# One tile of 1024 columns for the two exponent banks of a sequence, and new orders of the steps on four engines

## What is computed

```python
xn = layernorm(x)
z, xBC, dt = split(xn @ W_in)                   # 512, 768, 8 columns
dt = softplus(dt + dt_bias)
xBC = silu(causal_conv(xBC, conv_w, conv_b))    # 4 taps along the tokens
x_, B, C = split(xBC)                           # 8 heads of 64; state of 128
# per chunk of tokens, L[t, s] = exp(sum of dt*a between s and t), 0 for s > t
Y_diag = (C B^T * L) @ (x_ * dt)                # inside a chunk
Y_off  = C @ state * exp(cumsum)                # from the chunks before
y = (Y_diag + Y_off + x_ * D) * silu(z)
y = rmsnorm(y) * rms_w
h = xn + y @ W_out
out = x + layernorm(h) * ln_g + ln_b + tanh(xn @ F1 @ F2 @ F3 + bias)
```

## Time and profile before

| | before |
|---|---|
| median of 3 runs | 858.38 us (854.18 to 859.85) |
| the profiled execution | 857.2 us, its span 855.5 us |
| PE busy | 800.8 us, 94% |
| DVE busy | 726.5 us, 85% |
| ACT busy | 681.3 us, 80% |
| POOL busy | 702.0 us, 82% |
| mean granted TensorE clock | 0.976 |

### The profile page before, as it was taken

How to read it: one execution, slowest core, us unless ns; L and a number is a source line. 1 busy time by engine, 2 the same in 40 slices (tenths; PEclk the granted TensorE clock), 3 DMA queues, 4 the chain that set the end, 5 groups by cost and what they waited for, 6 DMA issues and landing times.

```text
span 855.5 us, 18389 instructions
## 1 busy us (share of the span) xinstructions
PE 800.8 (94%) x4944; PEld 671.5 (78%) x4944; DVE 726.5 (85%) x1826; ACT 681.3 (80%) x1767; POOL 702.0 (82%) x1096
## 2 busy tenths in 40 slices
PE   1479999999999999999999999999999999999974
PEld 1368888888888888888888888888888888888753
DVE  1669899998999999899999999999999998998741
ACT  1169888898888888988888889888888898888841
POOL 4036888898888889988888899888888988888884
PEclk9689999999999999999999999999999999999986
DMA  5000000000000000000000000000000000000000
GB/s 174 0 1 13 14 26 26 26 11 14 25 25 25 25 25 25 6 19 25 25 25 25 25 25 1 24 25 25 25 25 25 25 0 24 25 25 13 14 13 25
DMA packets 20848, 19.98 MB, mean 23 GB/s; under 512 B 2646, under 2 KB 20568, under 8 KB 20824
## 3 DMA queue, kind: packets, MB, share of 16 engines
q1 hardware_dynamic: 20824, 19.71, 7.2%
HBM read 11.31 MB, written 8.39 MB: 23 GB/s over the span
## 4 chain that ended last, share of the span: by engine, by line
POOL 39%; DVE 25%; issue 17%; PE 13%; ACT 2%; SPq 2%; POOLq 1%; DVEq 1%; DMA 0%; ACTq 0%
DVE u L624 7%; POOL xw L446 7%; PE ring L1012 5%; POOL obuf L491 4%; POOL left L434 3%; POOL sdec L453 3%; POOL xd L461 3%; POOL rs L483 3%; DVE pa L646 3%; POOL right L430 3%; DVE lay L677 3%; POOL obuf L493 3%; POOL btg L441 2%; DVE lay L683 2%; PE yoff_bank L1149 2%
## 5 line engine op out<-in xcount | busy, mean ns | idle before, releaser
L624 DVE SCALAR_TENSOR_TENSOR u<-ring,cw,u 128x256 f32<-128x256 f32 x576 | 260.5, 469 | 30.4 <-ACT u L847 29.8
L1012 PE MATMUL ring<-xhl,wh 128*128 128x262 f32 x768 | 174.8, 319 | 3.4 <-DVE u L624 3.4
L1012 PE MATMUL ring<-wh,xhl 128*128 128x512 f32 (+1 forms) x512 | 164.1, 374 | 3.3 <-DVE u L624 3.3
L1012 PEld LDWEIGHTS ring<-xhl,wh 128*128 128x128 f32 x768 | 124.7, 193 | 43.6 <-DVE u L624 21.6
L847 ACT ACTIVATE u<-ring,cb,cw 128x256 f32<-128x256 f32 x192 | 107.9, 562 | 45.6 <-PE ring L1012 40.9
L907 ACT ACTIVATE xdt<-xsb,dts 128x64 f32<-128x64 f32 x512 | 128.5, 335 | 0.0
L1131 PE MATMUL yd_bank<-xdt,lay 128*128 128x64 f32 x1024 | 123.2, 274 | 0.9 <-ACT yts L916 0.9
L1149 PE MATMUL yoff_bank<-wo,yts 128*128 128x256 f32 x512 | 122.1, 382 | 1.1 <-ACT yts L916 0.7
L1131 PEld LDWEIGHTS yd_bank<-xdt,lay 128*128 128x128 f32 x1024 | 121.2, 194 | 1.7 <-ACT yts L916 1.3
L1012 PE MATMUL ring<-xhl,wl 128*128 128x262 f32 x384 | 110.2, 287 | 0.0
L1012 PEld LDWEIGHTS ring<-wh,xhl 128*128 128x128 f32 x512 | 93.9, 192 | 20.0 <-issue 7.2
(11 more groups left out here) (134 smaller groups left out, 1995.7 us busy)
## 6 DMA issues: line engine op xcount, KB each, us to landing
xin<-in_x_dram SPq DMA_DIRECT2D x32, 256.0 KB, 2.9
out_dram<-obuf SPq DMA_DIRECT2D x32, 256.0 KB, 2.8
lay<-in_w_in_dram SPq DMA_DIRECT2D x1, 1288.0 KB
wo<-in_w_out_dram SPq DMA_DIRECT2D x1, 512.0 KB
lay<-in_f1t_dram SPq DMA_DIRECT2D x1, 256.0 KB
lay<-in_f2t_dram SPq DMA_DIRECT2D x1, 256.0 KB
lay<-in_f_dram SPq DMA_DIRECT2D x1, 256.0 KB
lng<-in_ln_g_dram SPq DMA_DIRECT2D x1, 128.0 KB
```

Source lines behind the costliest of these rows:

```text
L624: v.scalar_tensor_tensor(out=u[:, ct], in0=conv_bank(ct)[:, :, t:t + P], scalar=cw[:, ct, t:t + 1], in1=u[:, ct], op0=ALU.mult, op1=ALU.ad ...
L1012: last = mul(out, a, c, start=first and i == 0, stop=i == n - 1)
```

## The change

The two banks become one PSUM tile `e_pair` of 2 x 512 columns. `exponents` fills both halves and signals once, `decay` is one exponential over 1024 columns, `weigh` is one instruction over 1024 columns, and each waits for the whole pair. The semaphores have one instance per sequence in place of two. All four `one_pass` functions list their steps in a new order. No other instruction is added or taken away.

```diff
+        e_pair = ctx.enter_context(nc.psum_tensor("e_pair", [P, 2, 512], F32))
+        e_bank = [e_pair[:, 0], e_pair[:, 1]]
...
-                v.scalar_tensor_tensor(out=mm[:, q, hs], in0=e_bank[half][:, :].rearrange("p (j t) -> p j t", t=P), scalar=1.0,
-                                       in1=btg[:, q, P:2 * P].unsqueeze(1).to_broadcast([P, 4, P]),
-                                       op0=ALU.min, op1=ALU.mult).then_inc(m_done[q][half], 1)
+                v.scalar_tensor_tensor(out=mm[:, q], in0=e_pair[:, :, :].rearrange("p a (j t) -> p (a j) t", t=P), scalar=1.0,
+                                       in1=btg[:, q, P:2 * P].unsqueeze(1).to_broadcast([P, H, P]),
+                                       op0=ALU.min, op1=ALU.mult).then_inc(m_done[q], 1)
...
-                s.activation(e_bank[half][:, :], e_bank[half][:, :], ACT.Exp).then_inc(e_done[q][half], 1)
+            def decay(k, q):
+                act.wait_ge(e_in_psum[q], k + 1)
+                s.activation(e_pair[:, :, :], e_pair[:, :, :], ACT.Exp).then_inc(e_done[q], 1)
...
                 if begun(k - 1 + q):
-                    pe.wait_ge(m_done[1 - q][half], k + q)
-                bank = e_bank[half]
-                mul(bank[:, :], left[:, 2 * q + half], right[:, :, :].rearrange("p j t -> p (j t)"), start=True, stop=True)\
-                    .then_inc(e_in_psum[q][half], 1)
+                    pe.wait_ge(m_done[1 - q], k + q)
+                for half, bank in enumerate(e_bank):
+                    last = mul(bank[:, :], left[:, 2 * q + half], right[:, :, :].rearrange("p j t -> p (j t)"), start=True, stop=True)
+                last.then_inc(e_in_psum[q], 1)
...
                 pe.wait_ge(xdt_done[q], k + 1)
+                pe.wait_ge(m_done[q], k + 1)
                 for h in range(H):
-                    if h % 4 == 0:
-                        pe.wait_ge(m_done[q][h // 4], k + 1)
...
             def one_pass(k, b):
-                b1, bo = (b + 1) % BUF, (b - 1) % BUF
+                b1, b2, bo = (b + 1) % BUF, (b + 2) % BUF, (b - 1) % BUF
                 if live(k - 1):
                     scale_x(k - 1, 1)
-                if live(k + 1):
-                    halo(k + 1, b1)
+                if live(k):
+                    residual(k, b)
+                    residual_bias(k, b)
+                    spread_rows(k)
```

More of the change, by code:

```diff
@@ L216, in program @@
                 "mv2_done", "ve2_done", "rs2_done", "shift2_done", "hn_done", "hg_done", "out_done"))
-        e_in_psum, e_done, m_done = ([sems(f"{n}{q}_", 2) for q in range(Q)] for n in ("e_in_psum", "e_done", "m_done"))
+        e_in_psum, e_done, m_done = (sems(n, Q) for n in ("e_in_psum", "e_done", "m_done"))
         def begun(step):
@@ L528, in one_pass @@
                 if live(k):
-                    skip_x(k, 1)
+                    mask_g(k, 0)
+                    decay_state(k, b, 0)
                     add_skip(k, 0)
@@ L535, in one_pass @@
                     mask_g(k, 1)
+                if live(k - 1):
+                    last_norm_scale(k - 1, 0)
+                if live(k):
+                    skip_x(k, 1)
             passes(pool, one_pass)
@@ L669, in low_rows, with weigh @@
                 last.then_inc(rows_done, 1)
-            def weigh(k, q, half):
-                dve.wait_ge(e_done[q][half], k + 1)
+            def weigh(k, q):
+                dve.wait_ge(e_done[q], k + 1)
                 dve.wait_ge(g_done[q], k + 1)
@@ L751, in one_pass @@
                 if live(k):
-                    tap(k, 5, 2)
+                    softplus(k, b, 6)
+                    softplus(k, b, 7)
+                    softplus(k, b, 8)
                 if live(k + 1):
@@ L929, in one_pass @@
                 if live(k):
+                    conv_in(k, 4)
+                    conv_silu(k, b, 0)
+                if live(k - 2):
+                    last_apply(k - 2, 1)
+                if live(k - 1):
+                    b_and_g(k - 1, 1)
+                if live(k):
                     conv_in(k, 5)
-                    conv_silu(k, b, 0)
                 if live(k - 1):
@@ L952, in one_pass @@
                     branch(k + 1, 0)
+                    softplus_exp(k + 1)
+                if live(k - 1):
+                    y_channels(k - 1, 0)
                 if live(k):
@@ L957, in one_pass @@
                 if live(k - 1):
-                    y_channels(k - 1, 0)
+                    square(k - 1, 0)
+                if live(k - 2):
+                    last_apply(k - 2, 0)
                 if live(k + 1):
-                    softplus_exp(k + 1)
                     conv_in(k + 1, 0)
@@ L1174, in one_pass @@
                 if live(k - 2):
-                    transpose_y(k - 2, 1)
+                    out_project(k - 2, 1)
                 if live(k - 1):
-                    y_off(k - 1, bo, 0)
+                    x_tokens(k - 1, bo, 1)
                 if live(k):
@@ L1199, in one_pass @@
                     sums(k)
+                    x_tokens(k, b, 0)
                 if live(k + 1):
```

234 lines of the change are left out of this document (94 added, 140 removed).

## The result

The changed kernel takes 868.90 us in the median (867.65 to 869.51, 4 runs), the kernel before in the same comparison 856.77 (854.18 to 859.85): a ratio of 1.0138, interval [1.0098, 1.0179]. Its profiled execution took 868.63 us.

A forecast was written before the change was run, and what follows sets the result against it. The prediction took a chain of waits through POOL, ACT, PE and DVE, with DVE's stands on the shared port, to set a pass of 24.85 for 24.48 us; 857.2 + 0.37 x 31 gave 868.7, some 869 us, range 847 to 890.

The forecast's parts named there:

- the term of the sum: Growth of one pass from 24.48 to 24.85 us, +0.37 us, counted 31 times as +11.5 us.
- the walk: Nine steps once round the chain of waits, from POOL's `ve` through ACT, DVE and PE back to POOL: 24.85 us.
- Step 6: On DVE, `sv` meets POOL's `decay_state` and stands until 17.15; with `ww` and `pa` done at 17.75 us.
- Step 8: On DVE, `weigh`, held 0.1 by `mask_g`, ends at 23.2; `last_h` of sequence 1 and its statistics at 24.05 us.
- Step 9: On DVE, `pa` stands on POOL's `add_skip` until 24.3; with it, `mv` and the handover to POOL, 24.85 us.
- the two stands on the port: DVE's `sv` and `pa` waiting for large POOL instructions: 0.6 and 0.4 us of the pass, 23.85 without them.
- POOL's sum of 24.35: POOL's own instructions in the new order without the wait for `mv`: 24.35 us a pass, 0.13 less than before.
- steps 3 and 4: PE's six steps done at 9.7 us, then ACT's work from `branch` to `conv_in(0)` done at 13.5 us.
- The merge: One exponential on ACT and one weighing on DVE in place of two each: counted at 0 for the time.
- POOL alone: Rival: both stands of DVE fall away and POOL's own work sets the pass, -4 us, 853 us; chance 0.33.
- The shorter ends: Rival: waits outside the full passes shrink by some 10 us, with POOL's 24.35 in the loop, 843 us; chance 0.17.
- The third: Rival: each softplus of a DVE block waits anew, one more large POOL instruction per pass, 900 us; chance 0.08.

The follow-up runs named there:

- e2: Changed kernel with POOL's `mask_g` of sequence 0 moved ahead of `scale_x` of sequence 0: 863.62 us.
- e9: e2 with POOL's `decay_state(k-1, 1)` moved behind `layer_norm_scale(k+2)`: 862.82 us.
- e10: e9 with DVE's `last_mean_var(k-2, 1)` moved ahead of `softplus(k, b, 5)`: 860.33 us.
- e1: Changed kernel with the merge undone, two exponentials and two weighings per sequence again, in the new orders: 869.81 us.
- e5: Kernel before, in its old orders, with the merged exponential and weighing alone: 857.66 us.
- e12: e8 with the merged exponential and weighing added: 852.65 us in the median of nine executions.
- e8: Kernel before with POOL's `mask_g(k, 1)` moved ahead of `output(k-1, 1)`, into the wait for `last_apply`: 846.48 us, ratio 0.9871.
- e6: Changed kernel with the edits of e2 and e3 together, early mask and spread softplus: 870.66 us.
- e3: Changed kernel with DVE's softplus block (`sv`, `ww`, `pa`) taken apart and spread between the taps: 866.08 us.
- e11: e10 with POOL's `mask_g(k, 1)` moved into its wait for `last_apply`, and ACT's `b_and_g(k-1, 1)` ahead of `last_apply(k-2, 1)`: 848.56 us, ratio 0.9903.
- e4: Changed kernel with ACT's `last_apply(k-2, 1)` moved behind `conv_in(k, 5)`: 877.46 us.
- e7: e6 with POOL's `mask_g(k, 1)` moved into its wait for `last_apply`, and ACT's `b_and_g(k-1, 1)` ahead of `last_apply(k-2, 1)`: 856.87 us.

## Why the prediction was right, and where it was not

The time (869 for 868.9), the sign and the term of the sum, 0.37 us a pass, came out, and so did the walk's places. The causes put on the term did not, so that its size is luck in part. Counted from `ve` at 439.17 in the changed kernel's trace, forecast and measured:

| step | forecast | measured |
|---|---|---|
| 1, `conv_in(5)` done | 2.8 | 2.73 |
| 2, taps of tile 5 done | 4.3 | 4.29 |
| 3, PE done with what ACT's last branch needs | 9.7 | 9.70 |
| 4, ACT's `conv_in(0)` done | 13.5 | 13.45 |
| 5, statistics of sequence 0 done | 16.55 | 16.53 |
| 6, `sv`, `ww`, `pa` done | 17.75 | 17.54 |
| 7, DVE ready for `weigh` | 22.0 | 21.82 |
| `mask_g(0)` done | 22.1 | 22.02 |
| 8, statistics of sequence 1 done | 24.05 | 24.21 |
| 9, POOL's `ve` | 24.85 | 24.76 |

**Step 6** gave 0.6 us of the loss to `sv` on `decay_state`. The stand is there, from 455.62 to 456.30, with POOL's `sdec` ending at 456.27, and it costs nothing: after steps 6 and 7 DVE is ready 0.2 us before the mask, which ends where POOL's own row lengths put it. The prediction's own figures say so too: its step 8 starts `weigh` when the mask ends at 22.1, whenever `sv` is done. **Step 8** counted the mask as a hold of 0.1; it is 0.30, and it is what joins POOL to DVE: the path runs on POOL to 461.19 and on DVE to `mv`. The chain shows this link:

```profile
460.74 0.25 POOL btg L441
460.99 0.30 issue
461.29 0.81 DVE lay L673
```

**Step 9** had `pa` stand 0.4 us on `add_skip`. In the changed kernel `pa` starts at 463.29 and `add_skip` ends at 463.44, so it takes 0.18. The mask's hold brings DVE to `pa` when only 0.15 us of `add_skip` are left; e2 and e9 show `pa` at 0.46 and 0.75 as soon as DVE is earlier. The walk came out at 24.85 for 24.76 because it too starts `weigh` at the mask's end and had the mask's place within 0.1 us. The 0.2 us too many for `sv`, `ww` and `pa` were swallowed by that hold, and the 0.16 us by which the statistics of sequence 1 came later than forecast by the stand given to `pa`, which ends at 24.30, as forecast.

The statement "the two stands on the port are 0.6 and 0.4 us of that; without them the walk is 23.85" doesn't follow from the steps. `sv` would run from 16.55 to 17.15 and `pa` from 24.05 to 24.3; less their own 0.17 us the stands are 0.43 and 0.08, not 0.6 and 0.4; and with `weigh` held until 22.1 only the second could shorten the walk. The runs agree: without the mask's hold the pass was 24.57 (e2), with the stand of `sv` gone as well it stayed there (e9), and without any wait for `mv` (e10) it was 24.52. POOL's sum of 24.35 met e2's 24.57 less 0.24 of waiting, 24.33, but the `rs` in it had before's 0.63 us, and e2's has 0.54; where POOL waits for no `mv`, the pass is the 24.52 of e10.

So the loss has three parts. In the 27 middle distances the changed kernel loses 9.6 us against before, e2 5.0 and e10 2.8: 4.6 us go with the mask's hold, 2.2 with the edits of e9 and e10, which let `mv` come before POOL is ready for it, and 2.8 stay although POOL no longer waits. The prediction's sum over POOL made the pass 0.13 us shorter than before in that case; in the mean it is 0.10 longer.

Smaller slips: the terms written down in steps 3 and 4 give 9.6 and, from 9.7, 13.4 and not 9.7 and 13.5, since the handovers between engines (0.15 us from DVE's last tap to PE's `transpose_x`) aren't among them; and 868.7 is 1.2% above the median of 858.38, not 1.3%.

**The signs.** What the prediction named as showing it right came nearly all: `left` after 24.76 us, `sv` with a mean of 0.72, POOL's wait for `mv` of 0.48, ACT's of 0.96 ahead of `hh`. None of these signs tells the two causes apart; only an edit that takes one of them away does.

**The merge** at 0 holds (e1, e5). The exponential of 1024 columns took 1.01 us for the 0.95 forecast, the weighing 1.22 for 1.10, both within the bounds given. It does not hold where PE is the bound: there it costs 6 us in the median (e12 against e8, whose intervals against before touch at 0.9907), though not in each execution.

**The rivals.** POOL alone (853) fell by the wait for `mv`, and without that wait the kernel still takes 860 us (e10). The shorter ends fell: 102.1 us for 102.2; POOL's last long wait, 4.82 us for `mv` in the earlier trace rows, is now one of 3.82 for ACT's `junk` and one of 3.21 for `mv`. The third, each softplus waiting anew, was not so in the changed kernel (`ww` and `pa` 0.20 and 0.18 in the mean), but came in e6, by instructions set apart rather than side by side.

**The lock.** Every stand shown here ends 0.02 to 0.04 us behind a large POOL instruction: `sv` in the changed kernel, `pa` in e2 and e9, `ww` and `pa` in e3 and e6, `den` and `sv` in e12. `sv` beside the two-column `rs` in e9 took 0.16. The Trainium skill, "SBUF — State Buffer", section "SBUF: two separate sides", says that the shared port pair is an exclusive lock held for the whole instruction, and names for DVE an instruction with two inputs in SBUF. These rows agree for the large instructions. For POOL's power instruction over two columns they do not: it too reads SBUF, and by that rule `sv` would have waited in e9 for the end of `rs` at 452.51; it was done at 451.95, and `ww` and `pa` behind it by 452.37. The measurement decides: in these rows that instruction does not hold the pair for its whole length.

## What to carry to other kernels

A pass of a pipelined loop is set by a ring of waits over several engines; a stand on a port costs only if nothing later in the same walk waits for something slower. Before a stall is priced, ask which instruction behind it waits for another engine, and when that engine is done by its own work. And look for a gap of the engine that leads the chain: one independent instruction moved into POOL's 0.80 us round trip was worth 10.8 us in the old orders (e8) and, with a swap on ACT, 11.8 in the new (e11 against e10). And look again at an edit's own trace: spreading the softplus block (e3) was to take a stand away and only moved it.

## What was not expected of the hardware

- Three dependent 16-column instructions side by side stood once, 0.48 us (e2); set apart between taps they stood twice, 1.07 us (e6). Side by side they had only POOL's small `ve` and `rs` behind the large instruction; what a large one there would do, no run shows.
- The changed kernel's distances of `left` repeat in threes, 24.76, 24.75, 24.94 us, and e1 to e4, e6, e7, e9 and e10 the same way, where before's go 24.42, 24.49, 24.55. In the longer pass POOL's wait for `hh` is 0.94 for 0.80 us and that before `shift` 0.27 for 0.21. Some 2 us of the 11.5 lie there; why wasn't tried.
- POOL's `rs` of one column has 0.54 us with little beside it and 0.64 beside DVE's small `pb`, which has two inputs in SBUF (e10); whether `pb` is the cause wasn't tried.
